# A two-layer transformer kernel on one core: scores, masks and maxima in four column strips of TensorE, group loads with three transfers under way, and the gates' chain in the first block

## The reference

```python
q = (x @ W_q).reshape(b, t, 16, 8).transpose(0, 2, 1, 3)
...
scores = jnp.einsum('bhqd,bhkd->bhqk', q, k) / jnp.sqrt(jnp.float32(8))
scores = jnp.where(causal[None, None], scores, -jnp.inf)
attn = jax.nn.softmax(scores, axis=-1)
out = jnp.einsum('bhqk,bhkd->bhqd', attn, v)
...
ga = (2 * (ga >= 0) - 1) * jnp.maximum(jnp.abs(ga), 0.25)
x = x + ga * attention(h)
```

## Time and profile before

| | |
|---|---|
| time, median of 3 runs (lowest, highest) | 1459.21 us (1459.2, 1463.05) |
| the profiled execution's own time | 1468.58 us |
| its span, first to last instruction | 1466.7 us |
| busy: PE, DVE, ACT | 83%, 63%, 47% of the span |
| mean granted clock of PE | 0.892 of 2.4 GHz |

### The profile page before, as it was taken

One profiled execution on the slowest core, in us unless ns is written; L12 is line 12 of the kernel. 1 busy time (PEld: TensorE's weight loads), 2 busy tenths in 40 slices (PEclk: granted clock), 3 DMA queues, 4 the chain that ended last, 5 costly groups with the idle time before them and its releaser, 6 DMA issues. The chain is left out here.

```text
span 1466.7 us, 21010 instructions
## 1 busy us (share of the span) xinstructions
PE 1214.1 (83%) x7346; PEld 526.4 (36%) x7347; DVE 930.7 (63%) x2570; ACT 695.4 (47%) x928; POOL 235.3 (16%) x340
## 2 busy tenths in 40 slices
PE   6758999999999996069356999999989999485994
PEld 5322333333333334047222333333323343453663
DVE  5658888888688744001455888878868783442443
ACT  4323646666566673033232464656656667221331
POOL 2530000101000000735221000100100000063442
PEclk9668999999999997579667999999999999597997
DMA  3550000504120000121254101240400000011113
GB/s 129 151 74 16 16 16 17 84 16 63 37 75 3 3 2 1 47 66 50 83 150 60 32 33 32 53 65 2 58 13 2 4 3 2 1 44 41 48 48 106
DMA packets 43421, 63.98 MB, mean 44 GB/s; under 512 B 6816, under 2 KB 34624, under 8 KB 42128
## 3 DMA queue, kind: packets, MB, share of 16 engines
q0 software_dynamic: 7424, 24.00, 9.2%
q1 hardware_dynamic: 35904, 38.75, 9.2%
HBM read 45.42 MB, written 18.92 MB: 44 GB/s over the span
## 5 line engine op out<-in xcount | busy, mean ns | idle before, releaser
L943 ACT ACTIVATE probs_at<-st 128x1024 f32<-128x1024 f32 (+3 forms) x640 | 544.9, 896 | 404.4 <-PE st L898 278.3
L978 DVE TENSOR_REDUCE mxp_at<-mx 128x1 f32<-128x512 f32 x768 | 497.8, 685 | 118.2 <-PE mx L866 117.3
L866 PE MATMUL mx<-ks,qs 128*128 128x512 bf16 (+3 forms) x1280 | 384.7, 373 | 40.7 <-DMA ks<-k_parts 10.8
L898 PE MATMUL st<-qs,ks 128*128 128x512 bf16 (+3 forms) x1280 | 357.0, 356 | 32.7 <-DMA qs<-shrow_at 31.7
L914 PE MATMUL av<-probs_at,vs 128*32 128x512 f32 (+3 forms) x2560 | 300.9, 542 | 0.2
L980 DVE CUSTOM_DVE_ANT_0 junk_at<-mx,maskN 128x384 f32<-128x384 f32 (+3 forms) x512 | 241.4, 485 | 71.6 <-PE mx L866 69.7
L866 PEld LDWEIGHTS mx<-ks,qs 128*128 128x128 bf16 x1280 | 105.9, 99 | 395.1 <-DVE mxp_at L978 185.3
L898 PEld LDWEIGHTS st<-qs,ks 128*128 128x128 bf16 x1280 | 123.9, 100 | 135.6 <-DMA qs<-shrow_at 33.5
L1195 POOL DMA_INDIRECT perm<-rows,pos x64 | 63.1, 986 | 495.4 <-SPq L1304 242.3
L901 PE MATMUL st<-maskTb,identb 128*128 128x128 bf16 x512 | 100.1, 221 | 0.0
L914 PEld LDWEIGHTS av<-probs_at,vs 128*32 128x32 f32 x2560 | 50.6, 108 | 108.0 <-issue 97.0
(11 more groups left out here) (245 smaller groups left out, 1021.8 us busy)
## 6 DMA issues: line engine op xcount, KB each, us to landing
qs<-q_parts POOLq DMA_DIRECT2D x54, 128.0 KB, 4.1
ks<-k_parts POOLq DMA_DIRECT2D x18, 384.0 KB, 20.7
weights<-in_w_dram SPq DMA_DIRECT2D x16, 256.0 KB, 3.1
perm<-in_pad_dram SPq DMA_DIRECT2D x1, 2600.0 KB, 11.0
rows_f<-perm SPq DMA_DIRECT2D x39, 65.0 KB, 1.8
rows_f<-perm SPq DMA_DIRECT2D x8, 260.0 KB, 3.1
got_pj<-eo SPq DMA_DIRECT2D x4, 512.0 KB, 6.5
got_cb<-eo SPq DMA_DIRECT2D x4, 512.0 KB, 5.5
```

The source lines that it names most:

```text
L866: pe.matmul(buf[:, 0:w], QS[p][:, j, (4 * Q + qb) * P:(4 * Q + qb + 1) * P], KS[p][:, j, c * CH:c * CH + w], start=True, stop=True).then_i ...
L898: mm = pe.matmul(st[half][:, y, off:CH], KS[p][:, j, kb * P:(kb + 1) * P], QS[p][:, j, Q * CH + off:(Q + 1) * CH], start=True, stop=True, ...
L943: act.activation(probs[:, s % 2, 2 * half:2 * half + 2, off:CH], st[half][:, :, off:CH], ACT.Exp, scale=SCALE).then_inc(exp_done[half], 1)
L978: ins = v.tensor_reduce(dst, buf[:, 0:w], AX.X, ALU.max)
```

## The change

- In `rotate` (maxima) and `scores` (scores and masks), each matmul with 128 columns of weights becomes four with 32 columns, at tile positions (0, 0), (0, 32), (0, 64), (0, 96), each writing its 32 partitions of the same PSUM tile. The moving operand is the same for all four, N is unchanged, and only the last one signals. 3,072 matmuls (1,280 + 1,280 + 512) become 12,288.
- `load_group` issues the same 13 transfers in the same order, but from the fourth on POOL waits until the transfer three before has landed (three semaphores in turn). PE's wait for a group becomes three waits. POOL's copy of the group's values stands behind the loads, as before.
- The gates' chain moves from layer 0's attention to the end of DVE's work in `open_first`; it uses a free piece of KS's second buffer for the sign; PE's wait for `wo_ready` goes.
- The planner's costs of masks (0.11 to 0.09 for a half) and of group 1's loading (40 to 45) change; the order that comes out is the same but for one maxima matmul in each layer, which stands four steps later.

```diff
-    loaded = [0.0, 40.0] + [1e9] * NG
+    loaded = [0.0, 45.0] + [1e9] * NG
...
-            pe += 2 * w / 2400 + (.11 if STEPS[s][2] >= TPC * STEPS[s][1] else 0)
+            pe += 2 * w / 2400 + (.09 if STEPS[s][2] >= TPC * STEPS[s][1] else 0)
...
+                v.wait_ge(rows_out, 1)
+                g2, s2 = m.gates[:].rearrange("p a d -> p (a d)"), sign
+                v.tensor_scalar(s2, g2, 0., 2., ALU.is_ge, ALU.mult).then_inc(gates.sem, 1)
...
+                for l in range(2):
+                    v.tensor_tensor(m.wo[l], m.wo[l], m.gates[:, 2 * l], ALU.mult).then_inc(weights_ready, 1)
...
+UNDER_WAY = 3
+PER_SEM = [len(range(z, LOADS, UNDER_WAY)) for z in range(UNDER_WAY)]
...
-def load_group(eng, m, L, dram, g, done):
-
-    clear_shift(eng, m, dram, g % 2, done)
-    load_q(eng, m, L, dram, g, slice(0, T), done)
-    load_k(eng, m, L, dram, g, slice(0, T), done)
+def load_group(eng, m, L, dram, g, done, before):
...
+    for n, (dst, src) in enumerate(moves):
+        if n >= UNDER_WAY:
+            eng.wait_ge(done[n % UNDER_WAY], 16 * (before * PER_SEM[n % UNDER_WAY] + n // UNDER_WAY))
+        eng.dma_start(dst, src).then_inc(done[n % UNDER_WAY], 16)
...
-                                pe.wait_ge(kq_loaded[p], 16 * LOADS * (L * (1 + p) + (gg + 1) // 2))
+                                for z in range(UNDER_WAY):
+                                    pe.wait_ge(kq_loaded[p][z], 16 * PER_SEM[z] * (loads_before(gg) + 1))
...
-                        pe.matmul(buf[:, 0:w], QS[p][:, j, (4 * Q + qb) * P:(4 * Q + qb + 1) * P],
-                                  KS[p][:, j, c * CH:c * CH + w], start=True, stop=True).then_inc(mx_ready, 1)
+                        for z in range(0, P, 32):
+                            mm = pe.matmul(buf[z:z + 32, 0:w], QS[p][:, j, (4 * Q + qb) * P + z:(4 * Q + qb) * P + z + 32],
+                                           KS[p][:, j, c * CH:c * CH + w], start=True, stop=True, tile_position=(0, z), skip_group_check=True)
+                        mm.then_inc(mx_ready, 1)
...
-                        pe.wait_ge(wo_ready, 2)
...
-                        mm = pe.matmul(st[half][:, y, off:CH], KS[p][:, j, kb * P:(kb + 1) * P], QS[p][:, j, Q * CH + off:(Q + 1) * CH],
-                                       start=True, stop=True, skip_group_check=diag)
+                        for z in range(0, P, 32):
+                            mm = pe.matmul(st[half][z:z + 32, y, off:CH], KS[p][:, j, kb * P + z:kb * P + z + 32],
+                                           QS[p][:, j, Q * CH + off:(Q + 1) * CH], start=True, stop=True, tile_position=(0, z), skip_group_check=True)
                         if diag:
-                            mm = pe.matmul(st[half][:, y, off:off + P], m.identb[:], m.maskTb[:], start=False, stop=True, skip_group_check=True)
+                            for z in range(0, P, 32):
+                                mm = pe.matmul(st[half][z:z + 32, y, off:off + P], m.identb[:, z:z + 32], m.maskTb[:],
+                                               start=False, stop=True, tile_position=(0, z), skip_group_check=True)
```

More of the change, by code:

```diff
@@ L185, in open_first @@
         xn, hT = free_q[:, 0:T].rearrange("p (b d) -> p b d", d=D), free_q[:, T:2 * T]
-        mod = free_k[:, 0:W_MOD]
+        mod, sign = free_k[:, 0:W_MOD], free_k[:, W_MOD:W_MOD + 4 * D]
         cen, sq = (free_k[:, W_MOD + 8 * D + i * CH:W_MOD + 8 * D + (i + 1) * CH].rearrange("p (b l) -> p b l", l=LAT) for i in range(2))
@@ L470, in _ @@
                 residue(NS - 1)
+                v.wait_ge(rows_out, 1)
+                g2, s2 = m.gates[:].rearrange("p a d -> p (a d)"), sign
+                v.tensor_scalar(s2, g2, 0., 2., ALU.is_ge, ALU.mult).then_inc(gates.sem, 1)
+                v.wait_ge(gates.sem, gates.next())
+                v.tensor_scalar(s2, s2, -1., None, ALU.add).then_inc(gates.sem, 1)
+                v.wait_ge(gates.sem, gates.next())
+                v.tensor_tensor(g2, g2, s2, ALU.mult).then_inc(gates.sem, 1)
+                v.wait_ge(gates.sem, gates.next())
+                v.tensor_scalar(g2, g2, .25, None, ALU.max).then_inc(gates.sem, 1)
+                v.wait_ge(gates.sem, gates.next())
+                v.tensor_tensor(g2, g2, s2, ALU.mult).then_inc(gates.sem, 1)
+                v.wait_ge(gates.sem, gates.next())
+                for l in range(2):
+                    v.tensor_tensor(m.wo[l], m.wo[l], m.gates[:, 2 * l], ALU.mult).then_inc(weights_ready, 1)
             @block.gpsimd
@@ L732, in load_k @@
             [[H * T, 3 * HD], [T, GH], [1, cols.stop - cols.start]])).then_inc(done, 16)
-def load_group(eng, m, L, dram, g, done):
-    clear_shift(eng, m, dram, g % 2, done)
-    load_q(eng, m, L, dram, g, slice(0, T), done)
-    load_k(eng, m, L, dram, g, slice(0, T), done)
+def load_group(eng, m, L, dram, g, done, before):
+    q, k = (dram[f"{n}_parts{L}"].tensor for n in "qk")
+    moves = [(m.QS[g % 2][SHIFT0:SHIFT0 + 2 * GH], bass.AP(dram["zrow"].tensor, 0, [[T, 2 * GH], [0, GH], [1, T]]))]
+    for a in range(3):
+        for b in range(3):
+            r = (3 * a + b) * HD
+            moves.append((m.QS[g % 2][r:r + HD], bass.AP(q, (a * P + g * GH) * T, [[H * T, HD], [T, GH], [1, T]])))
+    for a in range(3):
+        r = 3 * a * HD
+        moves.append((m.KS[g % 2][r:r + 3 * HD], bass.AP(k, g * GH * T, [[H * T, 3 * HD], [T, GH], [1, T]])))
+    for n, (dst, src) in enumerate(moves):
+        if n >= UNDER_WAY:
+            eng.wait_ge(done[n % UNDER_WAY], 16 * (before * PER_SEM[n % UNDER_WAY] + n // UNDER_WAY))
+        eng.dma_start(dst, src).then_inc(done[n % UNDER_WAY], 16)
 def load_rows(sp, m, L, dram, got):
@@ L776, in attention @@
         weights_in = s_("weights_in")
-        kq_loaded = [s_(f"kq_loaded{p}") for p in range(2)]
+        kq_loaded = [[s_(f"kq_loaded{p}_{z}") for z in range(UNDER_WAY)] for p in range(2)]
+        loads_before = lambda g: L * (1 + g % 2) + (g + 1) // 2 - 1
         v_copied = [s_(f"v_copied{p}") for p in range(2)]
@@ L783, in attention @@
             "av_done", "av_free", "max_final", "hi_split", "mx_ready", "mx_free", "shift_split", "shift_row"))
-        rec_ready, wo_ready, gates = s_("rec_ready"), s_("wo_ready"), Count(s_("gates_chain"))
+        rec_ready = s_("rec_ready")
         RB, SB, UB = L * NROT, L * NST, L * NU
@@ L831, in _ @@
                 g.wait_ge(shift_set[0], 16 * (L * (NU // 4) + 1))
-                load_group(g, m, L, dram, 1, kq_loaded[1])
+                load_group(g, m, L, dram, 1, kq_loaded[1], loads_before(1))
                 if L == 0:
@@ L952, in _ @@
                     v.sem_inc(mx_free, MXBUF)
-                def finish_gates():
-                    g2, s2 = m.gates[:].rearrange("p a d -> p (a d)"), junk[:, 0]
-                    v.tensor_scalar(s2, g2, 0., 2., ALU.is_ge, ALU.mult).then_inc(gates.sem, 1)
-                    v.wait_ge(gates.sem, gates.next())
-                    v.tensor_scalar(s2, s2, -1., None, ALU.add).then_inc(gates.sem, 1)
-                    v.wait_ge(gates.sem, gates.next())
-                    v.tensor_tensor(g2, g2, s2, ALU.mult).then_inc(gates.sem, 1)
-                    v.wait_ge(gates.sem, gates.next())
-                    v.tensor_scalar(g2, g2, .25, None, ALU.max).then_inc(gates.sem, 1)
-                    v.wait_ge(gates.sem, gates.next())
-                    v.tensor_tensor(g2, g2, s2, ALU.mult).then_inc(gates.sem, 1)
-                    v.wait_ge(gates.sem, gates.next())
-                    for l in range(2):
-                        v.tensor_tensor(m.wo[l], m.wo[l], m.gates[:, 2 * l], ALU.mult).then_inc(wo_ready, 1)
                 for k, (kind, x) in enumerate(ROT):
                     buf = mxb[k % MXBUF]
-                    if L == 0 and (kind, x) == ("turn", 2):
-                        finish_gates()
                     v.wait_ge(mx_ready, RB + k + 1)
```

4 lines of the change are left out of this document (2 added, 2 removed).

## The result

The changed kernel takes 1389.61 us (median of 4 runs, 1388.09 to 1396.21) where the kernel before, beside it, takes 1459.95 us (4 runs, 1459.2 to 1463.05): a ratio of 0.9512, 95% interval 0.9486 to 0.9538, 70 us less. The profiled execution took 1390.73 us with a span of 1388.8 us, so 77.9 us less than the span of 1466.7 before. The forecast was 1418 us; the range began at 1388.

A forecast was written before the change was run, and what follows sets the result against it. PE was taken to set the pace, with DVE second. Strips −38, gates' chain −3 and loads 0 sum to −41 us, from the median 1459.2 to 1418 us; range 1388 to 1457 us.

The forecast's parts named there:

- A width change costs 0.09 us; 54 us gross: On PE in attention, 598 fewer changes of weight width at 0.09 us each save 54 us of PE time.
- The remainder of 0.025 us a group: 0.02 to 0.03 us beyond the stream in output passes; as first load costs streams nothing, paid by each group adds 77 us.
- every group pays: Rival, chance 0.10: each maxima, scores and mask strip group on PE pays 0.025 us again, giving 1489 us.
- exposed loads: Rival, chance 0.01: a strip's weights load only when PE's array is free, 332 us less 54, giving 1737 us.
- Prices (a), (b), (c): Strip costs on PE: last strip ending late, 6 us; first loads exposed after waits, 4; N = 128 matmuls, 8.
- Part 1: Four strips in maxima, scores and masks on PE, saving width changes: −38 us, from −56 to +33.
- The two long shift waits, −5: PE's two long waits for shift transfers during group loads shrink, together gaining 5 us, bounds 0 and 14.
- Four places give back 5 us: At four places in the last loads of both layers PE arrives 1.2 us sooner and waits, returning 5 us.
- Part 3: Group loads with three transfers under way: −5 + 5 = 0 us, from −23 to +21.
- PE cannot take the instructions (+270 us): Rival, chance 0.02: at 0.10 us a pair of load and matmul an ordinary step takes 4 us, +270 us.
- The clock, left as it is: PE's granted mean clock in attention, 0.94 and 0.92 of 2.4 GHz, was left unchanged in the forecast.
- better than forecast: Case, chance 0.10: strips cost nothing and group loads do not get longer, −56 − 3 − 9 = −68, 1391 us.

The follow-up runs named there:

- gates alone: The kernel before with only the gates' chain moved to the end of `open_first`: 1470.32 us, ratio 0.9975 to the kernel before.
- the changed kernel again: The changed kernel, unaltered, measured again on another chip beside the runs with other transfer limits: 1404.61 us, ratio 0.9522 to the kernel before.
- the strips of 64: The changed kernel with two strips of 64 columns in place of four of 32 in maxima, scores and masks, outputs staying at 32: 1462.3 us, ratio 0.9911.
- strips alone: The kernel before with only the four strips in scores, maxima and masks; loads, gates' chain and planner as before: 1440.2 us, ratio 0.9758.
- the loads alone: The kernel before with only the limit of three transfers under way, full-width matmuls and gates as before: 1453.26 us, ratio 0.9852.
- the halves: The changed kernel with maxima and scores also cut into column halves of at most 256, 8,192 more pairs of load and matmul: 1411.85 us, ratio 0.9579.

## Why the prediction was right in sign, and 28 us too careful

- **A width change costs 0.09 us; 54 us gross**: right. The trace after has 272 fewer changes a layer in steps 11 to 159, 544 × 0.09 = 49 us, and these steps lost 53.8 us. Read from the earlier trace rows, the 0.09 was confirmed by the table above, 78 to 100 ns on the mean (0.11 where PE does not wait). The few us over 49 may be clock: gates alone and the changed kernel again, with 27.4 us at 1.2 GHz each in these steps, differ by 822.7 − 774.6 = 48.1 us, though on two chips.
- **The remainder of 0.025 us a group**, on which the sign hung: taken rightly as the first load after a change. It is gone with the changes: 0.86 us for two passes in the changed kernel, and back again in the strips of 64. The rival that every group pays (1489 us) is refuted: 0.215 to 0.22 us a group. So is that of exposed loads. The rule of the Trainium skill, "TensorE: Matmul & The Clock Gate", section on packing small matmuls, that weight loads overlap matmuls in flight only when their row group differs, does not hold here: column strips share the rows, and their loads are hidden even with N = 128 (0.05 to 0.06 us a group).
- **Prices (a), (b), (c) of 6, 4 and 8 us**: mis-sized; about nothing. Four strips start within some 10 ns, and steps 91 to 159 gained 10.6 us where 116 fewer changes at 0.09 us give 10.4. Part 1 is −48 to −54 us, not −38.
- **The gates' chain, −3**: right (3.3 us; 3.7 [1.5 to 5.7] measured alone). That it needs 3.3 us in the first block too was wrong, 5.1 us; the cover was long enough.
- **The two long shift waits, −5 (bounds 0 and −14)**: the largest miss. 13.04 + 10.63 us became 2.39 + 2.04, −19 us, outside my bounds. The step that failed: "when what is left is mainly the keys' three transfers". I took the load's state before, with all 13 queued. Under the limit the keys are issued only from 93.49 on, after the shift at 91.91; what lies ahead of it are queries of 128 KB, and it lands in 5.2 us.
- **Four places give back 5 us**: the key waits and small shift waits there were 1.73 + 2.69 + 3.20 = 7.6 us before and are 1.89 + 1.30 + 3.18 = 6.4 now: nothing was given back, since the loads are 2 to 3 us shorter. Part 3 is about −20, not 0.
- **PE cannot take the instructions (+270 us)**: refuted as a rate, since 0.027 us a pair is seen for a whole group and 0.037 over 164 us, both well under the 0.10 of the rival. But I had priced only PE's own rate. The supply of instruction blocks past queued transfers was not in the prediction at all; it costs 19.5 us in the kernel with strips alone, and only the limit of three, there for another reason as I had it, keeps it away.
- **The clock, left as it is**: a term at nothing that was not quite nothing. Steps 0 to 11 gained 25.6 us, of which 19.2 are the shift's waits and 3.3 the chain; the 3 us left are the changes there and 20.9 us less at 1.2 GHz, not separated.

With the terms as measured: −48 to −54, −3, −20 is −71 to −77, against −77.9 between the spans and −70.3 between the medians. That the time fell inside the range owes much to luck: 1389.6 us is 1.6 us from its lower end, and the range's terms did not hold the gain of the shift. What came true is nearest to the case called better than forecast (1391 us, chance 0.10), in part for a reason that it did not hold, the shift waits.

## What to carry to other kernels

Where one kind of matmul must stand in a strip of the array, put all kinds that alternate with it into strips of the same width: count the changes in the order, at 0.08 to 0.11 us each, and leave no single one out. Cutting matmuls into strips multiplies the instructions, and instructions arrive by DMA; limit how many bulk transfers are queued at once, because a small transfer (15.9 us in place of 5.2) or an instruction block (16.5 to 17.2 us apart in place of at most 10) comes late while many are queued. The limit is a narrow optimum (here two cost 12 us and five 27, nearly as much as no limit), so try its neighbours.

## What was not expected of the hardware

- PE stopped for 4.3 to 5.6 us in the middle of a strip group at the second and third load of both layers, when no 16 KB block of instructions had come for 16.5 to 17.2 us under 13 queued transfers. With three under way the changed kernel has no such stop over 0.9 us, the loads alone have one of 1.09, and the halves, which need a block each 4.7 us, have 11.2 us in all.
- A change between two widths below 128, 64 and 32 columns, costs as much as one between 128 and 32: 100 and 91 ns on the mean. In an uninterrupted stream a change costs 0.10 to 0.115 us, the same beside scores of 128 as of 512 columns.
- Pairs of weight load and matmul with 32 columns stream at 0.027 us each with N = 256, and four with N = 128 in 0.05 to 0.06 us, some 0.014 us each.
- The same two DVE operations on 128x512 took 1.38 and 1.26 us at the end of the first block and 0.42 and 0.43 us in attention. It is not the place alone: the chain's other operation of this kind (L480), 2 us later, took 0.43 us. The two slow ones are those that write the piece of KS, the fast one works on `gates`. What slows them was not tried.
- Loads of 2.4 MB take 27 to 31 us with three transfers under way, 34 to 36 with two, 30 to 33 with five and 29 to 34 with all 13 queued: more in flight than three brings nothing.
